# Three base rounds in place of four in a neighbour-maximum kernel, with the side work of a group spread over twelve uses

## What is computed

```python
h = jnp.maximum(_layernorm(x, axis=-1), 0.0)
# inside the layer, with X = h and S = 25
pri = -jnp.arange(N, dtype=jnp.float32)
scores = jnp.where(mask, pri, neg_inf)
vals, idx = jax.lax.top_k(scores, S)                    # the 25 lowest neighbours
feats = jax.vmap(lambda x, i: x[i])(X, idx)
agg = jnp.where(valid[..., None], feats, neg_inf).max(axis=2)
agg = jnp.where((degree <= S)[..., None], jnp.maximum(agg, 0.0), agg)
out = jax.nn.relu(jnp.einsum('bnf,fo->bno', jnp.concatenate([X, agg], -1), W) + b)
x = x + out
```

## Time and profile before

| | |
|---|---|
| median of 3 runs | 662.07 us (659.44 to 663.03) |
| the profiled execution's own time | 664.44 us |
| its span in the profile | 661.5 us |
| TensorE busy | 596.5 us, 90% of the span, 2800 matmuls |
| VectorE busy | 597.0 us, 90%, 731 instructions |
| ScalarE busy | 401.7 us, 61% |
| GpSimd busy | 96.3 us, 15% |
| mean granted TensorE clock | 0.98 |

### The profile page before, as it was taken

How to read it: one execution, slowest core, us unless ns; L and a number is a source line. 1 busy time by engine, 2 the same in 40 slices (tenths; PEclk the granted TensorE clock), 3 DMA queues, 4 the chain that set the end, 5 groups by cost and what they waited for, 6 DMA issues and landing times.

```text
span 661.5 us, 9819 instructions
## 1 busy us (share of the span) xinstructions
PE 596.5 (90%) x2800; PEld 249.8 (38%) x2800; DVE 597.0 (90%) x731; ACT 401.7 (61%) x552; POOL 96.3 (15%) x142
## 2 busy tenths in 40 slices
PE   4678979899998999999998999999998999999886
PEld 2213333343434334343433444343433434343423
DVE  4965969999998999999999999999999999999996
ACT  3346837767486756858577666858477664846210
POOL 1400005000060002400060002400060000500000
PEclk9968989999999999999999999999999999999998
DMA  8745875858259593567558485567558262231100
GB/s 342 233 116 204 322 190 205 218 158 274 55 210 231 184 241 121 193 166 250 166 206 237 146 248 174 190 160 266 149 211 237 99 184 64 91 149 34 47 16 16
DMA packets 99437, 115.79 MB, mean 175 GB/s; under 512 B 66003, under 2 KB 85718, under 8 KB 94934
## 3 DMA queue, kind: packets, MB, share of 16 engines
q1 hardware_dynamic: 98262, 114.46, 55.6%
q10 hardware_dynamic: 1152, 1.05, 0.5%
HBM read 58.85 MB, written 20.97 MB: 121 GB/s over the span
## 4 chain that ended last, share of the span: by engine, by line
PE 53%; DVE 23%; issue 10%; DMA 5%; ACT 5%; SPq 2%; DVEq 1%; ACTq 0%
PE picked L639 17%; PE picked L640 15%; PE ring L568 9%; DVE best L827 8%; DVE late_hot L839 5%; DVE best L833 4%; PE final L666 2%; PE side L597 2%; PE side L596 2%; PE final L670 2%; DMA late_skew<-late 2%; DVE hot L814 2%; PE final L620 1%; DMA kept<-chosen 1%; ACT late L480 1%
## 5 line engine op out<-in xcount | busy, mean ns | idle before, releaser
L827 DVE TENSOR_TENSOR best<-picked,best 128x1024 f32<-128x1024 f32 x224 | 270.0, 1218 | 23.3 <-PE picked L640 21.9
L639 PE MATMUL picked<-hot,h_hi 128*128 128x512 f16 x512 | 196.6, 384 | 11.9 <-DVE best L833 6.8
L640 PE MATMUL picked<-hot,h_lo 128*128 128x512 f16 x512 | 195.9, 383 | 0.0
L639 PE MATMUL picked<-late_hot,hi_skew 128*128 128x512 f16 x344 | 130.5, 379 | 19.3 <-DVE late_hot L839 10.9
L640 PE MATMUL picked<-late_hot,lo_skew 128*128 128x512 f16 x344 | 130.3, 379 | 0.0
L833 DVE TENSOR_TENSOR best<-picked,best 128x1024 f32<-128x1024 f32 x86 | 105.0, 1221 | 15.4 <-PE picked L640 14.9
L467 ACT ACTIVATE late_rank<-ring,late_bias 128x512 bf16<-128x512 f32 x128 | 81.9, 686 | 60.4 <-PE ring L568 60.1
L467 ACT ACTIVATE rank<-ring,late_bias 128x512 bf16<-128x512 f32 x120 | 82.5, 688 | 49.0 <-PE ring L568 48.8
L475 ACT ACTIVATE chosen<-side,bias_cut 128x512 bf16<-128x512 f32 x120 | 81.9, 682 | 16.7 <-PE side L597 16.7
L498 ACT COPY best<-picked 128x1024 f32<-128x1024 f32 x32 | 32.4, 1013 | 85.3 <-PE picked L640 85.3
L639 PEld LDWEIGHTS picked<-hot,h_hi 128*128 128x128 f16 x512 | 50.4, 99 | 86.0 <-DVE best L827 15.5
(11 more groups left out here) (89 smaller groups left out, 490.9 us busy)
## 6 DMA issues: line engine op xcount, KB each, us to landing
adj_in<-in_adj_dram SPq DMA_DIRECT2D x15, 2048.0 KB, 8.6
picks<-kept SPq DMA_DIRECT2D x15, 1024.0 KB, 5.0
kept<-chosen SPq DMA_DIRECT2D x112, 128.0 KB, 3.1
late_skew<-late SPq DMA_DIRECT2D x32, 192.0 KB, 4.0
x_in<-in_x_dram SPq DMA_DIRECT2D x8, 512.0 KB, 6.3
late_skew<-late SPq DMA_DIRECT2D x16, 256.0 KB, 4.8
late_skew<-late SPq DMA_DIRECT2D x32, 128.0 KB, 3.6
xres<-in_x_dram SPq DMA_DIRECT2D x16, 256.0 KB, 2.7
```

The source lines that it names most:

```text
L639: nc.tensor.matmul(dst, hi[:, slot, k, :], onehot, start=start, stop=False)
L640: return nc.tensor.matmul(dst, lo[:, slot, k, :], onehot, start=False, stop=stop)
L827: nc.vector.tensor_tensor(best[:, half, s, :, :], picked[s][:, :, :], best[:, half, s, :, :], ALU.max).then_inc(picked_read, 1)
```

## The change

`BASE` goes from 4 to 3, so a group has 12 uses (0 to 11) and the late neighbours are those of rank 4 and up. The tables are drawn up anew: eight ranks go with uses 5 to 10 (were 6 to 13), eight choices with uses 6 to 11 (were 7 to 14), the count with 5 and 6, the first late compares with 8 and 9, the statistics with 7 and 8, the marks of the late ones all behind use 11. Six late ranks, not four, stand behind the loop, two behind use 1 and two behind each of uses 2 and 3, and the last two go with use 4. `make_hot(BASE, s)` at use 5 is gone, since ranks 2 and 3 are compared at the end of the step before. `make_gain` moves from use 5 of an odd group to the end of the even group before it.

```diff
-BASE = 4
+BASE = 3
...
-    SELECT_WITH, RANK_WITH = spread_over(7, 14), spread_over(6, 13)
-    LATE_EARLY, LATE_WITH, COUNT_WITH, COUNT_USE, LATE_HOT_USES = 4, {4: (4, 5), 5: (6, 7)}, (6, 7), 8, (13, 14)
-    LATE_USES, HIGH_USE, TURN_USE = {14: (0, 1), 15: (2, 3)}, 10, 15
-    STATS_USES, MOMENTS_USE, GAIN_USE = (9, 10), 12, 5
+    SELECT_WITH, RANK_WITH = spread_over(6, 11), spread_over(5, 10)
+    LATE_EARLY, LATE_WITH, COUNT_WITH, COUNT_USE, LATE_HOT_USES = 6, {4: (6, 7)}, (5, 6), 7, (8, 9)
+    LATE_USES, HIGH_USE, TURN_USE = {11: (0, 1, 2, 3)}, 8, 11
+    STATS_USES, MOMENTS_USE = (7, 8), 9
...
                 if more:
-                    late_ranks(g + 1, at + LATE_AT, 0)
-                    late_ranks(g + 1, at + LATE_AT, 1)
-                    pick_pair(g + 1, 2, next_slot)
-                    late_ranks(g + 1, at + LATE_AT, 2)
-                    pick_pair(g + 1, 3, next_slot)
-                    late_ranks(g + 1, at + LATE_AT, 3)
+                    for k in (0, 1):
+                        late_ranks(g + 1, at + LATE_AT, k)
+                    for use in (2, 3):
+                        pick_pair(g + 1, use, next_slot)
+                        for k in (2 * use - 2, 2 * use - 1):
+                            late_ranks(g + 1, at + LATE_AT, k)
                 project(g, it, u)
...
                     take_pair(g, use, s)
-                    if use == 5:
-                        make_hot(BASE, s)
-                    if use == GAIN_USE and more and u % PER_BATCH == PER_BATCH - 1:
-                        make_gain(batch_of(it, u + 1))
...
                 if more:
                     take_pair(g + 1, 3, 1 - s)
+                if ahead:
+                    make_gain(batch_of(it, u) + 1)
                 finish_group(g, s, 16 * (it * (UNROLL // 2) + u // 2 + 1))
```

More of the change, by code:

```diff
@@ L67, in build @@
     TURNED = 16 * Q
-    assert C == P and K == 8 and PER_BATCH == 2 and BASE == 4
+    assert C == P and K == 8 and PER_BATCH == 2 and BASE == 3
     LANDED = 16 * K
```

## The result

| | before | after |
|---|---|---|
| median of 4 runs | 661.59 us (659.44 to 663.03) | 730.69 us (728.93 to 731.25) |
| the profiled execution's own time | 664.44 us | 731.25 us |
| its span | 661.5 us | 729.5 us |
| mean granted TensorE clock | 0.98 | 0.98 |

The change makes the kernel slower: the ratio is 1.104, 95% interval 1.101 to 1.107. The forecast was +63 us, and the two spans differ by 68.0.

What follows compares the result with a forecast made beforehand. VectorE paces the loop, TensorE's queue and waits bound most uses, TensorE is late in the tail. Rounds +90.2 us, groups 0 to 13 -17.5, groups 14 and 15 -10.8, start +1: +63, taken as 724 us, range 708 to 738.

Steps and rivals of the forecast that it cites:

- Rounds: Late loops: 23 more rounds, 66 and not 43, at 3.92 us each, +90.2 us, all on the path.
- What the removed round gives back: Uses: at most 5.9 us a group; with TensorE's queue and waits only 1.3 us even and 3.2 us odd.
- The waits walked out from the earlier trace: TensorE in the uses waits for ScalarE's choices and ahead of the transposes: 2.9 us in odd groups, 3.8 in even.
- The even uses: From first use to the loop's first maximum in even groups: 20.3 us against 21.57, so 1.3 us back.
- rival 2: Uses: the waits are hidden but TensorE's slots are not, 47 us less than forecast, 677 us; chance 6%.
- The odd uses: From first use to the loop's first maximum in odd groups: 18.2 us against 21.42, so 3.2 us back.
- The tail: Fold to `finish_group`: more late ranks ahead of `project` and a second wait, +1.0 us a group with a successor.
- The start and the last two groups: Start: two more late ranks ahead of first use 4, +1 us. Groups 14 and 15: VectorE bounds their uses, -10.8 us together.
- VectorE does not keep the bound: Judges the rival that VectorE still bounds the uses, every group giving back 5.9 us: 658 us; chance 3%.
- The skew does not land behind the loop: Judges the rival that the late skew lands behind odd loops, short by 2 us in eight groups: 740 us; chance 10%.
- The clock did not fall: Judges the rival that TensorE falls to 1.2 GHz in uses 6 to 11: 864 us; chance 3%.
- VectorE's busy time: A sign over the whole span: it should fall slightly, 23 rounds x 3.99 us against 16 x 6.1.

Runs made afterwards that it cites:

- e2: The changed kernel with one late round less in every group, 50 rounds and not 66: 682.78 us, ratio 1.029.
- e5: The kernel before the change with one late round more per group, except one group that stayed at two: 717.52 us, ratio 1.085.
- e1: The changed kernel with eight ranks and eight choices spread evenly, one of each to each of uses 4 to 11: 723.4 us, ratio 1.093.
- e11: The changed kernel with e1's spread, e6's places for the first late compares and e8's early read together: 708.37 us, ratio 1.073.
- e8: The changed kernel with TensorE reading the number of late rounds ahead of use 11, not at the loop: 725.84 us, ratio 1.097.
- e4: The changed kernel with four late ranks behind the loop, as before, the other four with uses 4 and 5: 732.64 us, ratio 1.106.
- e3: The changed kernel with the first late compares at uses 6 and 7, not 8 and 9: 730.26 us, ratio 1.102.
- e6: The changed kernel with e1's even spread and the first late compares at uses 6 and 7: 712.35 us, ratio 1.077.

## Why the prediction was right, and where it was off

- **Rounds: right.** 66 rounds at 3.92 us each. It said that nothing waits beside the loop that is slower. e2 and e5 show that this was not quite so: behind loops of two rounds, and behind group 0's of three, the late skew was the later one. The waits stood in the earlier trace rows, and the sum forgot to take them off; with what follows from them they were 5.5 us.
- **What the removed round gives back: right in kind.** TensorE's queue and ScalarE's hand-over bound the uses, not VectorE. The waits walked out from the earlier trace rows, 1.3, 0.4, 0.95, 0.25 and 0.9 us, came out at 1.30, 0.37, 0.95, 0.22 and 0.95 when counted in slots. The even uses gave back 1.15 us (forecast 1.3). e1 shows that the order makes these waits, and also that rival 2, which has them hidden, would not have given 47 us: with most of them gone the kernel gains 7, since VectorE is next; with the long compare and the read out of the way too, e11 gains 22.
- **The odd uses: the term that was mis-sized.** 2.37 us came back, not 3.2. The step counted the loop's entry only in even groups, inside the 1.29 us with the transposes. In odd groups it took none, and there it is 0.87 us: from the first matmul of use 4 to the loop's first maximum a group takes 19.07 us (358.35 to 377.42), where 18.2 were worked out. Seven groups fell short by 0.83 us each, 5.8 us. e8 and e11 show that the gap is the read of the number of rounds.
- **The tail: right**, +1.01 us in each group, and e4 undoes it.
- **The start and the last two groups: off by 2 us each.** Group 0 was counted with a gain in its uses and +1, and its loop starts 1.75 us later (of which up to 1 us may be the start itself, which differs that much between executions: group 0's first hot compare of the loop is at 76.28 us before and at 75.35 in e5, which changes nothing ahead of it). Groups 14 and 15 come out at -9.0 together, not -10.8: without choices or without ranks their uses still give back only 5.0.
- **Sum.** +63 with +5.8 for the odd entries, +0.9 for the even uses, +2.0 for group 0, +1.8 for the last groups and -5.5 for the skew is +68. The two largest misses, +5.8 and -5.5, hid each other, which is luck; the rest is what the forecast fell short by.
- **The rivals.** VectorE does not keep the bound: the wait at choice 1 is 1.3 us, where under 0.3 was asked. The skew does not land behind the loop in the change; with a round less it does (e2). The clock did not fall. By the rule of the Trainium skill on short idles between groups of matmuls (TensorE: Matmul & The Clock Gate, "A second HAM failure mode: psum-queue depth-cycling") it might have, but the row from 316 to 329 us has 1.00 with five such idles of 0.2 to 1.3 us, and the trace does not bear the rule out for this kernel.
- **VectorE's busy time** was to fall by some 6 us and rose by 3. Most of the difference is one half compare in each of seven odd groups, which took 1.11 us before and 2.26 after, 8 us together. That is the last section's matter.

## What to carry to other kernels

Shifting work from a stretch where two engines are nearly full into a loop that one engine bounds cost the full price of the loop here; what came back was only what the second engine's queue let go, so walk that queue slot by slot before counting the first engine's savings. Side work for a third engine belongs one piece to a use: two pieces behind one another, both in need of that engine's answer, stall everything queued behind them by its round trip, here 1.3 us. Taking them apart is worth what the next wait leaves of it: 7 us here, and 22 with the two waits behind it. And count what a shorter loop had been hiding, and what a count that is read just ahead of a loop costs, though no row shows it.

## What had not been expected of the hardware

A half compare has a steady 0.74 us, and 2.26 beside GpSimd's subtraction. In an odd group of the change:

```profile
371.00 2.12 POOL L382 TENSOR_TENSOR h_lo<-h,h_hi 128x1024 f16<-128x1024 f32 x1
...
371.41 2.26 DVE L839 TENSOR_SCALAR late_hot<-late_rank,numbers 128x2048 f16<-128x2048 bf16 x1
```

The subtraction ends at 373.12 and the compare 0.55 us later, at 373.67. In e1 the same pair ends at 369.50 and 370.05, again 0.55 us apart. In the kernel before the compare started late in the subtraction and took 1.11:

```profile
344.58 2.12 POOL L382 TENSOR_TENSOR h_lo<-h,h_hi 128x1024 f16<-128x1024 f32 x1
...
346.14 1.11 DVE L839 TENSOR_SCALAR late_hot<-late_rank,numbers 128x2048 f16<-128x2048 bf16 x1
```

There too the ends are 0.55 us apart (346.70 and 347.25). In e3 the compare meets the last operation of GpSimd's normalization, and in e6 three maxima lie beside the subtraction:

```profile
361.00 2.78 POOL L400 TENSOR_SCALAR h<-h 128x1024 f32<-128x1024 f32 x1 [0.17 <-POOL h L397]
...
363.03 1.30 DVE L839 TENSOR_SCALAR late_hot<-late_rank,numbers 128x2048 f16<-128x2048 bf16 x1
```

```profile
360.94 3.57 DVE L827 TENSOR_TENSOR best<-picked,best 128x1024 f32<-128x1024 f32 x3
...
361.67 2.13 POOL L382 TENSOR_TENSOR h_lo<-h,h_hi 128x1024 f16<-128x1024 f32 x1
```

In e3 the ends are 363.78 and 364.33, once more 0.55 us apart, so it is not the subtraction alone that does it. The maxima lose nothing: three in a row take 3.57 us, the pace of the earlier trace rows. All but some 0.2 us of the compare's 0.74 are done after GpSimd's operation, however early the compare started. The Trainium skill (SBUF — State Buffer, "Who interferes with whom") says that VectorE, in its two-port modes, and GpSimd need the same pair of ports, which whichever issues first holds for its whole instruction while the other is fully blocked, and names `tensor_scalar`, the compare's operation, among those that can enter such a mode. The trace agrees in what it can show: 2.26 us, with the two ends 0.55 us apart each time; no row tells which mode the compare ran in. In e6, which moves the compare away, the half compares have a mean of 744 ns. It explains most of the rise of VectorE's busy time: what is counted as busy there is in part waiting.
